# Fetching the first head pair's operands inside the projection stage of a two-layer transformer kernel

## What is computed

```python
xn = layernorm(x)
q, k, v = split(xn @ Wqkv + bqkv, 3)                   # 16 heads of 32
scores = q @ k.T * scale + alibi_causal_bias
x = x + softmax(scores) @ v @ Wo + bo + ffn(xn)        # ffn: each token takes one of two experts
xn = layernorm(x)
x = x + lightning_attention(xn) + ternary_glu(xn)
```

## Time and profile before

| | |
|---|---|
| runs | 1883.82, 1884.2, 1897.36 us; median 1884.2 |
| profiled execution | 1884.51 us |
| its span | 1882.9 us (1.6 us lie around it) |
| busy: TensorE, VectorE, GpSimd, ScalarE | 90%, 50%, 34%, 31% |
| mean granted TensorE clock | 0.946 of 2.4 GHz |
| first stage | from 0 to the first DMA issue of the second at 169.93 us |

### The profile page before, as it was taken

One profiled execution on the slowest core, in us unless ns is written; L12 is line 12 of the kernel. 1 busy time (PEld: TensorE's weight loads), 2 busy tenths in 40 slices (PEclk: granted clock), 3 DMA queues, 4 the chain that ended last, 5 costly groups with the idle time before them and its releaser, 6 DMA issues. The chain is left out here.

```text
span 1882.9 us, 22883 instructions
## 1 busy us (share of the span) xinstructions
PE 1693.1 (90%) x8402; PEld 1100.1 (58%) x8402; DVE 939.9 (50%) x1575; ACT 590.2 (31%) x809; POOL 647.0 (34%) x527
## 2 busy tenths in 40 slices
PE   6996899999999999999697999939999995499997
PEld 5884444444444444443476777727767773388886
DVE  7653656566656566662243555535554543022322
ACT  3210145444444344445221212244323321122221
POOL 4000214768777886500135666523110100000000
PEclk9997599999999999999798999969999997799999
DMA  7756524543525353400462112143030210802210
GB/s 238 238 195 177 91 56 111 115 102 110 130 73 127 107 111 92 112 10 6 150 222 88 58 62 68 45 170 125 1 113 1 91 46 23 295 3 88 89 45 22
DMA packets 97589, 188.41 MB, mean 100 GB/s; under 512 B 26810, under 2 KB 36682, under 8 KB 95610
## 3 DMA queue, kind: packets, MB, share of 16 engines
q1 hardware_dynamic: 72350, 119.59, 22.4%
q0 software_dynamic: 13648, 51.61, 9.1%
q10 hardware_dynamic: 11488, 15.82, 2.6%
HBM read 121.84 MB, written 64.90 MB: 99 GB/s over the span
## 5 line engine op out<-in xcount | busy, mean ns | idle before, releaser
L925 DVE TENSOR_REDUCE att_maxes<-att_unit 128x1 f32<-128x512 f32 (+3 forms) x640 | 385.8, 611 | 261.2 <-PE att_unit L795 149.7
L907 ACT ACTIVATE att_probs<-att_scores 128x1024 f32<-128x1024 f32 (+1 forms) x320 | 285.3, 895 | 376.5 <-PE att_scores L824 185.8
L841 PE MATMUL att_outp<-att_probs,att_vs 128*64 128x512 f32 (+3 forms) x1280 | 307.6, 560 | 0.0
L795 PE MATMUL att_unit<-moew_wbh,moew_wah 100*128 100x512 f32 (+2 forms) x320 | 151.5, 490 | 9.4 <-DMA moew_wbh<-alibi_k_rounded 4.9
L1465 PE MATMUL glu_u<-glu_xh,glu_w 128*128 128x512 f32 x352 | 138.6, 394 | 18.9 <-DMA glu_xl<-zn_lo 18.9
L795 PE MATMUL att_unit<-moew_wbl,moew_wal 100*128 100x512 f32 (+2 forms) x320 | 138.2, 439 | 0.7
L1466 PE MATMUL glu_u<-glu_xl,glu_w 128*128 128x512 f32 x352 | 138.2, 393 | 0.0
L795 PEld LDWEIGHTS att_unit<-moew_wbh,moew_wah 100*128 100x128 f32 x320 | 66.7, 211 | 120.9 <-DVE att_maxes L925 80.7
L795 PEld LDWEIGHTS att_unit<-moew_wbl,moew_wal 100*128 100x128 f32 x320 | 60.1, 190 | 117.2 <-DVE att_maxes L925 81.7
L1524 DVE TENSOR_TENSOR glu_hid<-glu_sig,glu_u 128x512 f32<-128x512 f32 x44 | 30.2, 687 | 169.3 <-ACT glu_sig L1504 169.3
L1538 POOL DMA_DIRECT2D out<-glu_y x4 | 3.2, 790 | 312.5 <-DVE glu_y L1529 312.5
(11 more groups left out here) (276 smaller groups left out, 3454.8 us busy)
## 6 DMA issues: line engine op xcount, KB each, us to landing
att_q_raw<-in_w POOLq DMA_DIRECT2D x48, 352.0 KB, 3.9
w_ternary<-att_q_out POOLq DMA_DIRECT2D x24, 352.0 KB, 2.6
glu_w<-w_ternary ACTq DMA_DIRECT2D x9, 768.0 KB, 10.6
xn<-qkv_x SPq DMA_DIRECT2D x4, 1024.0 KB, 6.7
q_hi<-qkv_hi SPq DMA_DIRECT2D x16, 256.0 KB, 4.0
q_lo<-qkv_lo SPq DMA_DIRECT2D x16, 256.0 KB, 4.5
k_hi<-qkv_hi SPq DMA_DIRECT2D x16, 256.0 KB, 2.7
k_lo<-qkv_lo SPq DMA_DIRECT2D x16, 256.0 KB, 3.3
```

Of the source, the lines that this page charges most:

```text
L795: last = pe.matmul(unit[:, h, 0:cover], qs[par][0:SROWS, h, t * P:(t + 1) * P], ks[par][0:SROWS, h, g * CH:g * CH + cover], start=True, st ...
L841: last = pe.matmul(outp[v_cols(h), c % 2, off:CH], vs[p % 2][:, kt, v_cols(h)], probs[:, g % 4, h, off:CH], start=kt == 0, stop=kt == TT * ...
L907: act.activation(probs[:, g % 4, :, off:CH], scores[:, g % 2, :, off:CH], ACT.Exp).then_inc(exped, 1)
L925: dve.tensor_reduce(maxes[:, h, t, g:g + 1], unit[:, h, 0:width], AX.X, ALU.max).then_inc(unit_taken, 1)
```

## The change

1. A small class `Early` holds `wah`, `wbh`, `cst` and the three bf16 constants from the start of the program. The first stage's `xh` and `xl` now lie in slot 0 of `wah` and `wbh`, and pair 0's operands in slot 1.
2. The first stage issues, after the last key store of each chunk, the 8 loads of pair 0 for that chunk (3.2 MB in all, as before). Ahead of them SyncE waits for the stores of tiles 0 and 4 of the chunk (`qk_stored[0]`), and in chunk 0 also for both alibi stores (`al_stored`). The stage's end waits for the loads (`pair_in`).
3. The whole `cst` (192 KB) is loaded at the start in place of the identity alone (64 KB); VectorE makes the three bf16 constants in the first stage, after the low parts of chunk 0.
4. In the second stage `turned` and the strips of `vs` are filled by GpSimd; VectorE waits for the one before its first maximum, TensorE for the others before the first score. Pair 0's loads, `first_in` and the load of `cst` are gone.
5. `router.ranks` stands after the first 4 units.
6. The projection stage's load of the identity is gone; the experts use `cst`.

```diff
@@ class Early @@
+        self.wah, self.wbh = st.sb("wah", [P, 2, KT * FH], F32R), st.sb("wbh", [P, 2, KT * FH], F32R)
+        self.cst = st.sb("cst", [P, 3, P])
+        self.ident, self.neg_q, self.neg_k = (st.sb(n, [P, P], BF16) for n in ("ident", "neg_q", "neg_k"))
@@ normed_qkv_stage @@
-        xh = [st.sb(f"xh{i}", [P, KT, CH], F32R) for i in range(2)]
-        xl = [st.sb(f"xl{i}", [P, KT, CH], F32R) for i in range(2)]
+        xh, xl = ([t[:, 0, i * KT * CH:(i + 1) * KT * CH].rearrange("p (k t) -> p k t", k=KT) for i in range(2)]
+                  for t in (early.wah, early.wbh))
...
-            sp.dma_start(ident[:], cst_d[:, 0, :]).then_inc(ident_in, 16)
+            sp.dma_start(early.cst[:], cst_d).then_inc(ident_in, 16)
...
+                if c == 0:
+                    sp.wait_ge(al_stored, len(alibi) * 16)
+                sp.wait_ge(qk_stored[0], (c + 1) * 64)
+                t = slice(c * CH, (c + 1) * CH)
+                load_queries(sp, Early.operands(early.wah), 0, t, qh_d, ql_d, alibi[0][1], pair_in)
+                load_keys(sp, Early.operands(early.wbh), 0, t, kh_d, kl_d, alibi[1][1], pair_in)
                 sp.wait_ge(taken, (c + 1) * NP)
                 sp.dma_start(rows_of(v_d, c), vb[:]).then_inc(v_stored, 16)
...
-                    (qk_stored[i], NCH * 2 * NQK // 4) for i in range(4)] + [(v_stored, NCH)]:
+                    (qk_stored[i], NCH * 2 * NQK // 4) for i in range(4)] + [
+                    (v_stored, NCH), (pair_in, NCH * 2 * LOADS)]:
...
+            dve.wait_ge(ident_in, 16)
+            for i, t in enumerate((early.ident, early.neg_q, early.neg_k)):
+                dve.tensor_copy(t[:], early.cst[:, i, :]).then_inc(bf_ready, 1)
@@ attention_stage @@
-            for c in range(NCH):
-                t = slice(c * CH, (c + 1) * CH)
-                load_queries(0, t, first_in[c])
-                load_keys(0, t, first_in[c])
...
-                if p == 0 and t % TT == 0 and g == 0 and h == 0:
-                    pe.wait_ge(first_in[t // TT], 2 * LOADS * 16)
...
+                if g == 0:
+                    pe.wait_ge(ones_set, 2)
...
-            router.ranks(pe)
-            pe.wait_ge(cst_ready, 6)
             for v in range(LEAD):
+                if v == TT:
+                    router.ranks(pe)
...
-            act.dma_start(cst[:], cst_d).then_inc(cst_in, 16)
             router.load(act)
...
-            dve.memset(turned[:], 0.0).then_inc(cst_ready, 1)
-            for i in range(2):
-                dve.memset(vs[i][:].rearrange("p t (a b) -> p t a b", b=HD)[:, :, 0:4:3, :], 1.0).then_inc(cst_ready, 1)
-            dve.wait_ge(cst_in, 16)
-            dve.tensor_copy(ident[:], cst[:, 0, :]).then_inc(cst_ready, 1)
-            dve.tensor_copy(neg_q[:], cst[:, 1, :]).then_inc(cst_ready, 1)
-            dve.tensor_copy(neg_k[:], cst[:, 2, :]).then_inc(cst_ready, 1)
-            dve.wait_ge(cst_ready, 6)
+            dve.wait_ge(turned_set, 1)
...
+            pool.memset(turned[:], 0.0).then_inc(turned_set, 1)
+            for i in range(2):
+                pool.memset(vs[i][:].rearrange("p t (a b) -> p t a b", b=HD)[:, :, 0:4:3, :], 1.0).then_inc(ones_set, 1)
```

More of the change, by code:

```diff
@@ L348, in low, with __init__, operands, load_queries @@
                           ALU.subtract).then_inc(self.xl_ready, 1)
-def normed_qkv_stage(nc, w_d, bqk_d, bv_d, x_d, cst_d, wg_d, diff, xn_d, qh_d, ql_d, kh_d, kl_d, v_d, alibi):
+class Early:
+    def __init__(self, st):
+        self.wah, self.wbh = st.sb("wah", [P, 2, KT * FH], F32R), st.sb("wbh", [P, 2, KT * FH], F32R)
+        self.cst = st.sb("cst", [P, 3, P])
+        self.ident, self.neg_q, self.neg_k = (st.sb(n, [P, P], BF16) for n in ("ident", "neg_q", "neg_k"))
+    @staticmethod
+    def operands(t):
+        return t[0:KROWS, 1, :].rearrange("p (h t) -> p h t", h=2)
+def load_queries(eng, q, p, t, qh_d, ql_d, aq_d, arrived):
+    rows = slice(p * 2 * HD, (p + 1) * 2 * HD)
+    for b, q_d in enumerate((qh_d, ql_d, qh_d)):
+        eng.dma_start(q[b * HD:(b + 1) * HD, :, t].bitcast(F32),
+                      q_d[rows, t].rearrange("(h f) t -> f h t", h=2)).then_inc(arrived, 16)
+    eng.dma_start(q[QROWS:SROWS, :, t].bitcast(F32),
+                  aq_d[p * 8:p * 8 + 8, t].rearrange("(h r) t -> r h t", h=2)).then_inc(arrived, 16)
+def load_keys(eng, k, p, t, kh_d, kl_d, ak_d, arrived):
+    rows = slice(p * 2 * HD, (p + 1) * 2 * HD)
+    for b, k_d in enumerate((kh_d, kh_d, kl_d)):
+        eng.dma_start(k[b * HD:(b + 1) * HD, :, t].bitcast(F32),
+                      k_d[rows, t].rearrange("(h f) t -> f h t", h=2)).then_inc(arrived, 16)
+    eng.dma_start(k[QROWS:KROWS, :, t].bitcast(F32),
+                  ak_d[p * 12:p * 12 + 12, t].rearrange("(h r) t -> r h t", h=2)).then_inc(arrived, 16)
+LOADS = 4
+def normed_qkv_stage(nc, early, w_d, bqk_d, bv_d, x_d, cst_d, wg_d, diff, xn_d, qh_d, ql_d, kh_d, kl_d, v_d, alibi):
     NQK, NP = 2 * KT, 2 * KT + TT
@@ L672, in store, with attention_stage @@
         pool.wait_ge(self.idx_in, 16)
-def attention_stage(nc, cst_d, aq_d, ak_d, qh_d, ql_d, kh_d, kl_d, v_d, att_d, sum_d, rt, route_d, w, ahead, ternary):
+def attention_stage(nc, early, aq_d, ak_d, qh_d, ql_d, kh_d, kl_d, v_d, att_d, sum_d, rt, route_d, w, ahead, ternary):
     with Stage(nc, "att") as st:
-        cst = st.sb("cst", [P, 3, P])
-        ident = st.sb("ident", [P, P], BF16)
-        neg_q, neg_k = st.sb("neg_q", [P, P], BF16), st.sb("neg_k", [P, P], BF16)
-        qs, ks = ([t[0:KROWS, 1, :].rearrange("p (h t) -> p h t", h=2) for t in pair]
-                  for pair in ((w.wah, w.wal), (w.wbh, w.wbl)))
+        cst, ident, neg_q, neg_k = early.cst, early.ident, early.neg_q, early.neg_k
+        qs, ks = ([Early.operands(t) for t in pair] for pair in ((w.wah, w.wal), (w.wbh, w.wbl)))
         vs = [st.sb(f"vs{i}", [P, QT, 4 * HD]) for i in range(2)]
@@ L698, in attention_stage @@
         outp = st.ps("outp", [P, 2, CH])
-        cst_in, cst_ready = st.sem("cst_in"), st.sem("cst_ready")
-        first_in = [st.sem(f"first_in{c}") for c in range(NCH)]
+        turned_set, ones_set = st.sem("turned_set"), st.sem("ones_set")
         pair_in = [st.sem(f"pair_in{i}") for i in range(2)]
@@ L707, in attention_stage @@
         block = st.block()
-        LOADS = 4
         MAX_LINKS = 3
@@ L756, in store @@
                                  ).then_inc(stored[c % 2], 16)
-            for c in range(NCH):
-                t = slice(c * CH, (c + 1) * CH)
-                load_queries(0, t, first_in[c])
-                load_keys(0, t, first_in[c])
-            load_queries(1, early, pair_in[1])
-            load_queries(1, late, pair_in[1])
-            load_keys(1, whole, pair_in[1])
+            queries(1, first)
+            queries(1, late)
+            keys(1, whole)
             load_values(sp, 1)
@@ L770, in _ @@
                         sp.wait_ge(summed, p * NS)
-                        load_queries(p + 1, late, pair_in[(p + 1) % 2])
-                        load_keys(p + 1, whole, pair_in[(p + 1) % 2])
+                        queries(p + 1, late)
+                        keys(p + 1, whole)
                         load_values(sp, p + 1)
@@ L777, in _ @@
                     sp.wait_ge(scored, p * NS + NS - QT)
-                    load_queries(p + 2, early, pair_in[p % 2])
+                    queries(p + 2, first)
                 store(p, 2)
@@ L1224, in h_turn @@
                     for i in range(HT):
-                        last = pe.transpose(ht[:, half, i, :], g[:, half, i * P:(i + 1) * P], ident[:])
+                        last = pe.transpose(ht[:, half, i, :], g[:, half, i * P:(i + 1) * P], ident)
                     last.then_inc(h_turned, 1)
```

51 lines of the change are left out of this document (20 added, 31 removed).

## The result

| | before | after |
|---|---|---|
| median (22 runs each) | 1883.65 us | 1872.2 us |
| lowest and highest | 1874.33, 1900.56 | 1864.5, 1881.2 |
| ratio, 95% interval | | 0.994 (0.9922 to 0.9959) |
| profiled execution, span | 1884.51, 1882.9 | 1874.89, 1873.2 |

The ratio says 11.3 us saved, between 7.7 and 14.7. On another chip the changed kernel came out at 0.996 (0.993 to 0.9991), 7.6 us of 1895.

What follows compares the result with a forecast made beforehand. At the seam between the first two stages nothing computes: TensorE waits for constants and loads, and VectorE's maxima chain follows. -10.9 + 0.3 + 0.9 + 0.7 = -9.0 us from 1884.5 gives 1875.5, forecast 1875.4, range 1865 to 1881.

Steps and rivals of the forecast that it cites:

- two of the three signs: Wrong if first stage ends over 2 us later, step 0's score isn't 8 to 10 earlier, or clock's return shifts over 10.
- Pair 0's loads, -10.9: Seam: with chunk 0's operands on chip, first maximum at 171.35 instead of 182.28; chunks 1 to 3 were never waited for.
- GpSimd's fills, +0.3: Second stage's start: a GpSimd fill could hold the count's tensor_scalar on VectorE; +0.3 us, bounds 0 and +3.1.
- Ranks behind unit 3, +0.9: Second stage, between units 3 and 4: the ranks' 1.44 us of TensorE work is not fully hidden; +0.9, bounds 0 and +1.4.
- Three casts, +0.7: First stage, chunk 0: VectorE's casts beside GpSimd's work take 3.8 us, mostly absorbed by slack; +0.7, bounds 0 to +2.6.
- SyncE's backlog, 0: First stage: SyncE's stores come later and ScalarE waits until about 83.5, but TensorE loses 0, up to +3.
- rival B: First stage: SyncE's later stores reach TensorE and the casts cost 2.6, so the time is 1880.4; chance 0.09.
- The first stage unchanged but for the casts: First stage: only the casts' +0.7 counted; second stage's first DMA issue expected within 1 us of 169.9.
- The clock: After the seam: TensorE's return to 2.4 GHz, about 239 before, shifts with the work to near 230.
- Rival A: Seam: TensorE's clock doesn't fall to 1.2 GHz because its idle time halves; time 1863.8; chance 0.08.
- C: After the seam: the clock returns later, each us of delay costing 0.38; at 260 the time is 1887; chance 0.05.
- Rival A's price, 11.7 us: Seam and units after it: what TensorE's clock staying up would save beyond the forecast, giving 1863.8.

Runs made afterwards that it cites:

- Late fills: Changed kernel, but GpSimd's fills of `vs` wait for VectorE's count and the three casts stand in chunk 1 of the first stage: ratio to before 0.9923.
- chunk 0 alone early: Changed kernel, but only chunk 0's 8 loads stand in the first stage; those of chunks 1 to 3 are issued at the second stage's start: ratio to before 0.9966.
- all but the loads: Changed kernel with all of pair 0's loads back at the seam; constants, fills and ranks stay where the change put them: ratio to before 1.0004.
- ranks first: Changed kernel with the ranks back ahead of the first unit: ratio to before 0.9994.
- loads alone: Kernel before with only pair 0's loads moved early; fills, casts, `cst` and ranks as before: ratio to before 0.9965.
- Chunk 0's loads late: Changed kernel, but chunk 0's 8 loads of pair 0 are issued in chunk 1, ahead of that chunk's own: ratio to before 0.9933.
- busy matmuls: Matmuls whose result is never read, added around the seam to the kernel with late fills and casts: ratio 0.9928; with indirect DMAs also later: 0.9942.

## Why the prediction was right, and where not

The time (1875.4 forecast, 1872.2 measured) is right, and so is the main mechanism: the loads leave the seam, and the first stage pays little. But two of the three signs that the prediction gave of being wrong have come up. The score of step 0 is 10.9 us earlier (216.01 before, 205.15 now) and not 8 to 10, and the clock's return moved by some 12 us against the work and not by less than 10. By its steps:

- *Pair 0's loads, -10.9.* Late fills show it without other effects: first maximum at +1.38 from the start, against 12.35: 10.97. Right. "Chunks 1 to 3 were never waited for" is true of the trace, but it does not follow that their early loads are worth nothing: with chunk 0 alone early, unit 4 waits 2.52 us for chunk 1. A wait that does not show may be covered by the one that is removed.
- *GpSimd's fills, +0.3.* Mis-sized: the tensor_scalar was held for 1.69 - 0.17 = 1.5 us, inside the stated bounds (0 and 3.1). I let it start about when the short fill ends; the long fills stand right behind that one, so it met them. In all three profiles that show 1.69 us it ended with the second long fill; in three others (all but the loads, chunk 0 alone, ranks first) it took 0.80 and ended with the first.
- *Ranks behind unit 3, +0.9.* From first maximum to unit 4's maximum 6.57 us in place of 6.02: 0.6. Near enough; the constants were there in time. That the ranks ahead of the units would have cost 4.1 us I had not priced, though it was in the numbers.
- The seam: -10.9 + 1.5 + 0.6 = -8.8, measured -8.9.
- *Three casts, +0.7.* They took 0.98 + 1.32 + 1.32 = 3.6 us (forecast 3.8), but the delay was not worked off by VectorE "since its later work then falls behind GpSimd's end": the chunk was normalized 4.8 us later, not 3.8. What that costs depends on the first stage's clock. In the seven profiles with these casts the second stage begins at 167.8 to 168.5, whether the clock is back for good at 24.8 or at 27.2. Without them it begins at 165.7 (loads alone, clock back at 25.7) and at 167.2 (late fills and casts, 27.6). So the casts cost 0.8 us where the clock comes back as late as in the profile of the kernel before, and 2.3 us where it comes back early, inside the bounds (0 and 2.6). The rule quoted from the Trainium skill ("SBUF — State Buffer", "Who interferes with whom") holds at both places: late fills and casts bring 1.69 back to 0.17 and 1.32 to 0.22, with the same operations at times when GpSimd does not compute.
- *SyncE's backlog, 0.* Right, with its times: v store at 64.29 (forecast 64.5), x store at 64.73 (64.9), ScalarE until 82.97 (83.5). Chunk 0's loads late confirm it, so rival B falls.
- *The first stage unchanged but for the casts.* This step failed, and the sum lacks its term. The second stage began 1.9 us earlier in spite of the casts, since the matmuls run at another pace: a tile of chunk 3 takes 2.72 us in all twelve profiles of the changed kernel and its variants, and 2.80 in both with the first stage of the kernel before. Between profiles with the clock back at 27.6 in both and no casts in chunk 0, the stage is 2.7 us shorter (169.93 before, 167.19 with late fills and casts), and 2.7 - 0.8 = 1.9. The earlier clock of the profile after (2.4 GHz for 3.4 us from 18.2, and for good from 25.0) is not the reason: chunk 0's loads late had it back at 27.2 only and started the second stage at 168.02. Neither the early loads nor the casts make the pace, since all but the loads has it, and so has loads alone. What the twelve share is the place of the buffers in `Early` (item 1 of the change); no kernel changes that alone, so the cause stays open.
- *The clock.* Rival A (it does not fall) falls, and so does C. But the forecast let it return in step with the work, near 230; it came at 216. The step that failed is the anchor: the 239 of one profile. The kernel before showed 226 in another. In the ten profiles with the early loads or parts of the change it came back between 212 and 224 where no matmuls were added.
- *Rival A's price, 11.7 us.* In one profile the busy matmuls bring 10.6 us at exponential 60. In the medians, 12 runs of each, they bring 1.1 and, beside late fills and casts, 0.0005 of the ratio to the other side. Their mean clock is higher (0.953 against 0.944 and 0.945), and by clock and span that is 33 us less at 1.2 GHz. Where this goes in a typical run no profile here shows; it stays open.

Why 11.3 us and not 9.0? To the first exponential the profiled pair gained 10.9 us: 8.9 at the seam and 1.9 ahead of it. The sum was 1.2 us too good for the fills and lacked 2.7 us for the pace of the matmuls, so that two errors cancel in part. From there to the end of the program the places of the low-clock stretches decide: the profiled pair ends 9.7 us apart, and the two chips' ratios, 0.994 and 0.996, are 11.3 and 7.6. The close hit of the median is in part luck.

## What to carry to other kernels

Before pricing a wait that goes, list what else ends at the same place: here loads, constants and ranks each hid the other, and either half of the change alone brought a quarter or nothing. Small VectorE casts and tensor_scalars should be put where GpSimd is idle, and GpSimd's fills behind them; a placement costs nothing, and only the trace shows it. Read a clock's return or a low-clock stretch from several profiles before it anchors a number. And compare the pace of the work that the change leaves alone: here the same matmuls took 3% less time, 2.7 us that no step of the sum had.

## What the runs showed that I had not expected

Two things. First, VectorE and ScalarE stop while GpSimd issues its 16 indirect DMAs, though neither needs anything from them. Ten profiles of the changed kernel and its variants have these DMAs at about 205 to 240 us; in 8 of them VectorE stands 2 to 7 us at a time there, and ScalarE 4 to 10 (in the one profile of the kernel before, where they run at 1.2 GHz, VectorE has no stop of 2 us and ScalarE none over 3.4). In the three kernels with the indirect DMAs moved no such stop is left there, and in each one appears near the end of their new place (356.97 above), between 342 and 370 us, where VectorE has none of 2 us in the kernels that have them at the old place. Stops of this size are not theirs alone, though: all 14 profiles have one of ScalarE, of 4.5 to 8 us, somewhere between 300 and 342, while GpSimd issues none. The Trainium skill ("SBUF — State Buffer", "Who interferes with whom") states that ScalarE never waits on anyone and that a tensor_reduce does not contend on this chip. By it the port shared with GpSimd would not be the cause of the 8.19 us and 3.97 us above; no run here tests that, and the cause stays open.

Second, the spread. The time of a run goes with its mean granted clock: over the 31, 34 and 35 runs of the kernel before in the three groups the correlation is -0.77, -0.91 and -0.87, with 1.7, 2.0 and 1.9 us for each 0.001. Kernels with the same seam agree at the first exponential to 0.1 us (38.60, 38.62 and 38.62; 37.10 and 37.10), and at exponential 60 the same code differs by 12.5 us (177.0 and 189.5). An edit of 2 us, such as the late fills and casts, is read from the seam and not from the median.
